# Eight graphs through four message-passing layers on one core: a merge of four edits, with the weighted values ahead of the score products

## The chip, the cores and the metric

The kernel runs on one core of one Trainium2 chip. The metric is the device time of one execution, in microseconds (us). The kernel before takes 3336.92 us, the median of three runs (3333.25 to 3337.58). The core has five engines, each with its own instruction queue: PE (matrix products), DVE (vector), ACT (scalar functions), POOL (GpSimd) and SP, which here issues the DMAs. They meet through semaphores only.

## The reference, cut to what matters

Eight graphs (B = 8) of 1024 nodes with 256 features each pass four layers, each added to `x`:

```python
h = relu(layernorm(x)); x = x + L0(h, adj, nodemask)   # one softmax over the nodes, scales v = h @ Wv
h = relu(layernorm(x)); x = x + L1(h, adj, ...)        # 8 heads of 32: softmax(q k^T * scale * 2 adj) v, then Wo
h = relu(layernorm(x)); x = x + L2(h, adj, ...)        # hypergraph convolutions over (adj != 0)
h = relu(layernorm(x)); x = x + L3(h, adj, ...)        # adj * exp(q k^T), normalised, times v

# L0:  agg = adj @ k;  w = mask / sqrt(256) * sum_d(q * agg);  softmax(w)[:, None] * v
# L1, for one head:
scores = einsum('bhqd,bhkd->bhqk', q, k) * SCALE * (adj + adj)
attn = softmax(scores, axis=-1);  ctx = einsum('bhqk,bhkd->bhqd', attn, v);  out = ctx @ Wo.T + bo
```

Everything is float32.

## The kernel before, in words

The graphs are worked one after the other (`batch`). Seven of them are iterations of a loop in hardware (`Fori`) on DVE, ACT, POOL and SP, the eighth stands behind it as code of its own; PE has all eight in its loop. The order of the work is written out by hand, apart for each engine, and each engine waits on counting semaphores. Nothing is scheduled by a planner.

**The attention loop (L1)** is where most of the change lies. Its 64 *units* are 8 tiles of 128 queries by 8 heads. For a unit `u`:

- PE, `scores(u)`: two products of 128x512 into one of two pairs of PSUM banks (L1104). They are issued in step `u-2`, and wait until DVE has read the pair for unit `u-2`.
- DVE, L726: scores times adjacency into the buffer `Z` (one of three), and the row's maximum into `nm`. It issues in step `u`. DVE then negates that maximum (L731), since ACT adds it as a bias.
- ACT, L912: the exponential in place, with the row sums.
- PE, `transposes(u)`: eight 128x128 transposes of `Z` (L1124), issued in step `u`, into two of three banks that take turns.
- ACT (first half, L904) and DVE (second half, L683) copy them to `PT`, one or two steps later. In every fourth unit (`BOTH = 4`) ACT copies both halves.

Four units (four heads) form a *group* `g`. POOL spreads its inverse sums over columns (L496, `rs`), PE transposes them (`spread_inverses`, L1132, at the end of step 4g+5), and ACT copies the result to `Rs` at the start of step 4g+6 (L909). The weighted values (L1146, 32-column tiles of the array) follow in steps 4g+6 to 4g+8, in parts of 3, 3 and 2 of the 8 key tiles (`PARTS`). The first part waits for `Rs`, since both live in PSUM bank 7. DVE multiplies by `Rs` (L695). After every second group, PE applies the output weights (`project`, through the helper at L983), at the start of steps 8t+14. POOL also computes the 0/1 incidence `H` of a tile in one instruction (L505). The first units run while SP still stacks `kS` and `qS` by DMA.

In one step PE issues: `project` if due, scores of unit u+2, a part of weighted values if due, transposes of unit u, spreading if due:

```python
                    if u + 2 < UNITS:
                        scores(u + 2)
                    for part in range(len(PARTS)):
                        if (g := group_due(u, WEIGH + part)) is not None:
                            weighted_values(g, part)
                    if 0 < u < UNITS:
                        transposes(u)
```

**The start of a graph (L0).** PE transposes the first half of `h` (L1015), four pieces of the adjacency (L1031), and then the second half of `h`, for which it waits until DVE has copied the first half out of PSUM (L594). DVE comes to that copy after it has finished the previous graph. At L0's end the weights of 8 tiles are masked and scaled on DVE (L621), their maximum is taken (L623), broadcast (L625) and transposed by PE.

**From L2 to L3.** PE forms a product of two weight matrices (M3), runs two products whose result nobody reads (`keep_warm`, L1007), and waits for ACT's copy of M3 and for ACT's normalised `h` (L869). `h` waits on DVE's `shift`, which waits on POOL's power (`norm_scale`, L482 and L484); POOL starts this last one behind the layer's last product and a memset (L520).

Of the kernel before, what the change touches and what calls it, by code (L numbers as in the profile page):

```python
# [7 lines left out]
ALU = mybir.AluOpType  # L8
# [23 lines left out]
def build_program(nc, x_in, adj_in, mask_in, wqkT0, wv0, w1attn, bq1, bk1, bv1, bo1,  # L32
# [13 lines left out]
    BOTH = 4  # L46
# [7 lines left out]
    with ctx:  # L54
# [25 lines left out]
        mhalf = sb("mhalf", [P, NT])  # L80
        mask = sb("mask", [P, NT])
# [130 lines left out]
        chain = signal("chain", 9)  # L212
# [86 lines left out]
        PARTS = (3, 3, 2)  # L299
# [168 lines left out]
        def _(pool):  # L468
# [6 lines left out]
            pool.wait_ge(consts_ready.sem, 4)  # L475
# [10 lines left out]
            def batch(b, last):  # L486
# [3 lines left out]
                for g in range(NT * GROUPS):  # L490

                    pool.wait_ge(*invs(b, g + 1))
# [5 lines left out]
                    if g % GROUPS == GROUPS - 1:  # L498

                        t = g // GROUPS  # L500
                        pool.wait_ge(*zs(b, HEADS * (t + 1)))
                        if t == NT - 2:
                            norm_scale(b, 2, 0)
                        stand(pool, waited_pool)
                        pool.tensor_scalar(H[:, t], adjN[:, t], 0.0, 0.0, ALU.is_equal, ALU.is_equal).then_inc(Hs.sem, 1)  # L505
# [26 lines left out]
        def _(dve):  # L532
# [19 lines left out]
            dve.wait_ge(consts_ready.sem, 4)  # L552
# [43 lines left out]
            def batch(b, last):  # L596
# [15 lines left out]
                for t in range(NT):  # L612
                    dve.wait_ge(*agg_ps(b, t + 1))
# [6 lines left out]
                dve.wait_ge(*chain(b, 1))  # L620
                dve.tensor_tensor(sw[:, 1], sw[:, 0], mask16[:], ALU.mult).then_inc(chain.sem, 1)  # L621
                dve.wait_ge(*chain(b, 2))
                dve.reduce_max(s1[:, 0:1], sw[:, 1], AX.X).then_inc(chain.sem, 1)  # L623
                dve.wait_ge(*chain(b, 3))
                dve.tensor_copy(E3[:, 1, 0:P], s1[:, 0:1].broadcast_to([P, P])).then_inc(wm_bc.sem, 1)  # L625
# [3 lines left out]
                dve.reciprocal(s1[:, 3:4], ps[:, 5, 0:1]).then_inc(chain.sem, 1)  # L629
                dve.wait_ge(*chain(b, 4))  # L630
# [703 lines left out]
```

## Time and profile before

| | |
|---|---|
| median of three runs | 3336.92 us |
| the profiled execution | 3340.5 us, span 3337.7 us |
| mean granted PE clock | 0.986 of full speed |
| PE, matmul records | 3172.0 us busy, 95% of the span |
| DVE | 2040.6 us, 61% |
| ACT | 1524.3 us, 46% |
| POOL | 577.5 us, 17% |

A graph takes some 412 us, of which the attention loop is about 150. Shares over the whole span hide that DVE and ACT are idle in the long product stages and nearly full in the attention loop (in 600 to 650 us: PE 49.2, DVE 44.3, ACT 41.2 of 50 us). The records of matmuls overlap, as they are pipelined, so what a product costs PE is read from start to start of neighbouring rows, not from a row's duration. The profiled execution lies 3.6 us above the median.

### The profile page before, as it was taken

What the parts mean: (1) busy time and instruction counts of PE and PEld (TensorE: products, weight loads), DVE (VectorE), ACT (ScalarE), POOL (GpSimd) and SP (SyncE); (2) the same over time, 40 slices, a digit from 0 to 9 for tenths busy, and PEclk for the clock granted to TensorE, in tenths of its full rate; (3) what the DMA queues carried; (4) which work ended last, traced back from release to release, by engine and by line L of the source; (5) the groups of instructions that cost most, each with busy time, mean ns of one, the idle gap of its engine ahead of it and who ended that gap; (6) DMA issues with size and microseconds to landing.
All of it is one profiled execution on the core that took longest, in us unless ns stands there. A gap on an engine that the chain in (4) does not pass through costs nothing.

```text
span 3337.7 us, 64889 instructions
## 1 busy us (share of the span) xinstructions
PE 3172.0 (95%) x23656; PEld 2450.6 (73%) x23656; DVE 2040.6 (61%) x4913; ACT 1524.3 (46%) x2881; POOL 577.5 (17%) x400
## 2 busy tenths in 40 slices
PE   6899998999989999899998999989999899998999
PEld 5677786777867778677776786767867678676786
DVE  2688426884368843687436874378743786437863
ACT  1584215842158431684316833168322683227722
POOL 0123001230012300123001230012300122001320
PEclk8999999999999999999999999999999999999999
DMA  3301203012030020300203002030020301112000
GB/s 109 77 2 33 73 14 77 2 33 73 14 77 2 33 73 14 77 2 33 73 14 77 2 33 73 14 77 2 33 73 18 73 2 43 62 39 52 24 10 13
DMA packets 75103, 135.44 MB, mean 41 GB/s; under 512 B 8592, under 2 KB 43792, under 8 KB 74768
## 3 DMA queue, kind: packets, MB, share of 16 engines
q1 hardware_dynamic: 74768, 131.01, 13.9%
q8 instruction: 206, 3.38, 0.4%
q14 instruction: 129, 1.06, 0.1%
HBM read 72.26 MB, written 8.39 MB: 24 GB/s over the span
## 4 chain that ended last, share of the span: by engine, by line
PE 80%; SPq 7%; issue 4%; DVE 4%; ACT 3%; DMA 1%; POOL 0%; ACTq 0%; DVEq 0%; POOLq 0%
PE ps L983 35%; PE ps L1184 14%; PE ps L1124 14%; SPq L426 7%; PE ps L1146 6%; PE ps L1104 5%; PE ps L1031 2%; PE ps L1132 1%; ACT h L869 1%; DVE hT L594 1%; PE ps L1015 1%; ACT Z L912 1%; DMA qS<-qlo 1%; DVE stats L560 0%; ACT h2T L938 0%
## 5 line engine op out<-in xcount | busy, mean ns | idle before, releaser
L726 DVE CUSTOM_DVE_ANT_0 Z<-ps,adjN 128x1024 f32<-128x1024 f32 x512 | 621.2, 1213 | 64.9 <-PE ps L1104 47.3
L1124 PE MATMUL ps<-ident,Z 128*128 128x128 f32 x4096 | 569.7, 283 | 74.3 <-ACT Z L912 43.6
L912 ACT ACTIVATE Z<-Z,nm 128x1024 f32<-128x1024 f32 x512 | 587.4, 1147 | 29.5 <-DVE nm L731 27.6
L1124 PEld LDWEIGHTS ps<-ident,Z 128*128 128x128 f32 x4096 | 458.7, 143 | 188.6 <-issue 98.5
L904 ACT ACTIVATE PT<-ps 128x512 f32<-128x512 f32 x640 | 364.1, 590 | 84.5 <-PE ps L1124 47.7
L1104 PE MATMUL ps<-kS,qS 128*128 128x512 f32 x1024 | 374.0, 450 | 6.8 <-ACT qS L894 6.8
L1146 PE MATMUL ps<-PT,v 128*32 128x128 f32 x8192 | 303.9, 279 | 0.0
L1146 PEld LDWEIGHTS ps<-PT,v 128*32 128x32 f32 x8192 | 205.6, 110 | 131.9 <-issue 130.7
L683 DVE COPY PT<-ps 128x512 f32<-128x512 f32 x384 | 264.2, 688 | 41.6 <-DMA qS<-qlo 21.7
L496 POOL TENSOR_SCALAR rs<-sm 128x128 f32<-128x128 f32 x128 | 68.2, 533 | 1080.2 <-DVE sm L687 1080.2
L505 POOL TENSOR_SCALAR H<-adjN 128x1024 fp32r<-128x1024 f32 x64 | 233.4, 3646 | 0.0
L983 PE MATMUL ps<-v,P 128*128 128x257 f32 x1024 | 223.6, 380 | 0.0
L983 PE MATMUL ps<-mh,adjT 128*128 128x256 f32 x1024 | 222.3, 380 | 0.0
L983 PE MATMUL ps<-hT,t3T 128*128 128x512 f32 x512 | 221.0, 593 | 0.0
L983 PEld LDWEIGHTS ps<-v,P 128*128 128x128 f32 x1024 | 194.2, 190 | 31.5 <-issue 3.8
L983 PEld LDWEIGHTS ps<-mh,adjT 128*128 128x128 f32 x1024 | 195.1, 191 | 25.9
L482 POOL TENSOR_SCALAR ve<-mv 128x4 f32<-128x4 f32 x80 | 15.7, 197 | 1116.9 <-DVE mv L565 1115.4
L983 PEld LDWEIGHTS ps<-hT,t3T 128*128 128x128 f32 x512 | 97.5, 190 | 118.8 <-issue 118.4
L617 DVE CUSTOM_DVE_ANT_0 E<-ps,G 128x256 f32<-128x256 f32 x64 | 27.2, 425 | 246.5 <-PE ps L983 246.5
L1104 PEld LDWEIGHTS ps<-kS,qS 128*128 128x128 f32 x1024 | 165.8, 198 | 14.6 <-issue 10.0
L983 PE MATMUL ps<-W,hT 128*128 128x256 f32 x768 | 174.3, 381 | 0.0
L966 ACT ACTIVATE E<-ps,cj 128x512 f32<-128x512 f32 x128 | 87.9, 687 | 187.4 <-PE ps L983 187.4
(165 smaller groups left out, 5395.6 us busy)
## 6 DMA issues: line engine op xcount, KB each, us to landing
adjN<-adj_in SPq DMA_DIRECT2D x8, 4096.0 KB, 15.9
kS<-khi SPq DMA_DIRECT2D x48, 256.0 KB, 3.8
kS<-klo SPq DMA_DIRECT2D x48, 256.0 KB, 5.0
qS<-qhi SPq DMA_DIRECT2D x96, 128.0 KB, 3.0
qS<-qlo SPq DMA_DIRECT2D x96, 128.0 KB, 3.1
xn<-x_in SPq DMA_DIRECT2D x8, 1024.0 KB, 6.1
out<-x SPq DMA_DIRECT2D x8, 1024.0 KB, 4.9
W1h<-w1T SPq DMA_DIRECT2D x9, 512.0 KB, 5.7
```

The lines of the kernel that those rows point to most:

```text
L426: sp.dma_start(to.bitcast(F32), src[HD * j:HD * j + HD, :, cols].bitcast(F32)).then_inc(done.sem, 16)
L505: pool.tensor_scalar(H[:, t], adjN[:, t], 0.0, 0.0, ALU.is_equal, ALU.is_equal).then_inc(Hs.sem, 1)
L683: dve.tensor_copy(PT[:, u % PTS, NT // 2:NT], heads_of(ps[:, bank])).then_inc(PT_dve.sem, 1)
L726: dve.tensor_tensor_reduce(Z[:, u % ZS], ps[:, 2 * (u % 2):2 * (u % 2) + 2].rearrange("p a n -> p (a n)"), adjN[:, u // HEADS], SCORE_SCAL ...
L904: act.activation(PT[:, u % PTS, first:first + NT // 2], heads_of(ps[:, bank]), ACT.Copy).then_inc(PT_act.sem, 1)
L912: act.activation(Z[:, u % ZS], Z[:, u % ZS], ACT.Exp, bias=nm[:, u:u + 1], accum_out=sm[:, u:u + 1]).then_inc(exps.sem, 1)
L966: act.activation(E3[:, n % 2], ps[:, n % 4], ACT.Exp, bias=cj[:, n % NT:n % NT + 1]).then_inc(e3s.sem, 1)
L983: mm = pe.matmul(dst, lhsT, rhs, start=(i == 0), stop=(i == len(pairs) - 1))
L1104: mm = pe.matmul(ps[:, 2 * (u % 2) + s], qS[:, hd, rows(t)], kS[:, hd, half(s)], start=True, stop=True)
L1124: mm = pe.transpose(ps[:, turn_bank((u, s)), rows(a)], Z[:, u % ZS, rows(NT // 2 * s + a)], ident[:])
L1146: mm = pe.matmul(ps[HD * j:HD * j + HD, 7, 0:P], v[:, kt, HD * hd:HD * hd + HD], PT[:, (HPG * g + j) % PTS, kt], start=(kt == 0), stop=(kt ...
L1184: mm = pe.matmul(dst(n, i), lhs(n, j, i), rhs(n, j, i), start=(j == 0 and i == 0), stop=(j == NT - 1 and i == 0))
```

## The change

Six things change; the first three are in the attention loop.

1. In a step, PE issues the weighted values ahead of the scores of unit u+2, and they come in two parts of 4 key tiles instead of 3, 3 and 2.
2. The negation of the maxima goes from DVE to POOL (`negate_max`). POOL's order is now written by steps: negate, spread the inverse sums if due, one eighth of a tile's incidence.
3. ACT copies both halves in every sixth unit instead of every fourth; DVE takes the others.
4. L0's start: ACT makes the copies of transposed `h`. PE's second half of `h` waits for the masked `h` (`mhs`) instead of the copies.
5. L0's end: mask and scale are applied by ACT as it copies `G`; the maximum of seven tiles is taken while PE works on the eighth, and DVE then makes maximum and broadcast in one instruction.
6. From L2 to L3: POOL's power and DVE's `shift` of the first half come earlier, ACT normalises the first half ahead of its M3 copy, M3 uses another bank, and the two unread products are gone; the transposes of `h` no longer wait for M3's copy.

```diff
-    BOTH = 4
+    BOTH = 6
-        PARTS = (3, 3, 2)
+        PARTS = (NT // 2, NT // 2)
...
@@ POOL, attention loop
-                for g in range(NT * GROUPS):
...
-                        pool.tensor_scalar(H[:, t], adjN[:, t], 0.0, 0.0, ALU.is_equal, ALU.is_equal).then_inc(Hs.sem, 1)
+                def negate_max(u):
+                    pool.wait_ge(*zs(b, u + 1))
+                    pool.tensor_tensor(nm[:, u:u + 1], nm[:, u:u + 1], minus[:], ALU.mult).then_inc(nms.sem, 1)
...
+                def incidence(t, of):
+                    done = pool.tensor_scalar(H[:, t, of], adjN[:, t, of], 0.0, 0.0, ALU.is_equal, ALU.is_equal)
...
+                for u in range(STEPS):
+                    if u < UNITS:
+                        negate_max(u)
+                    if (g := group_due(u, INVERT)) is not None:
+                        spread_sums(g)
...
+                    if HEADS <= u < UNITS:
+                        incidence(u // HEADS - 1, rows(u % HEADS))
...
@@ POOL, L2 to L3
+                norm_scale(b, 4)
                 pool.wait_ge(*a4_ps(b, NT))
                 stand(pool, waited_pool)
                 pool.memset(v3[:, :, D:HW], 1.0).then_inc(ones_col.sem, 1)
-                norm_scale(b, 4)
@@ DVE, L0
-                hT_copies(b, 0, 0)
                 for n in range(1, NT * NH, 2):
-                    if n == 5:
-                        hT_copies(b, 0, 1)
...
-                dve.tensor_tensor(sw[:, 1], sw[:, 0], mask16[:], ALU.mult).then_inc(chain.sem, 1)
...
-                dve.tensor_copy(E3[:, 1, 0:P], s1[:, 0:1].broadcast_to([P, P])).then_inc(wm_bc.sem, 1)
+                dve.tensor_scalar(E3[:, 1, 0:P], sw[:, 0, NT - 1:NT].broadcast_to([P, P]), s1[:, 0:1], None,
+                                  ALU.max).then_inc(wm_bc.sem, 1)
@@ DVE, attention loop
-                    if u < UNITS:
-                        dve.wait_ge(*zs(b, u + 1))
-                        dve.tensor_scalar(nm[:, u:u + 1], nm[:, u:u + 1], -1.0, None, ALU.mult).then_inc(nms.sem, 1)
@@ ACT
+                hT_copies(0)
                 for n in range(0, NT * NH, 2):
+                    if n == 4:
+                        hT_copies(1)
...
+                normalise(b, 4, x, range(TPH))
                 act.wait_ge(*m3_ps(b, 1))
...
+                normalise(b, 4, x, range(TPH, NT))
@@ PE
-                        pe.wait_ge(*hTs(b, DT))
+                        pe.wait_ge(*mhs(b, NT))
                         transpose_h(b, 0, 1)
...
-                    if u + 2 < UNITS:
-                        scores(u + 2)
                     for part in range(len(PARTS)):
                         if (g := group_due(u, WEIGH + part)) is not None:
                             weighted_values(g, part)
+                    if u + 2 < UNITS:
+                        scores(u + 2)
...
-                keep_warm(bank(1), 2)
+                transpose_h(b, 2, 0)
                 pe.wait_ge(*m3s(b, 1))
-                transpose_h(b, 2, 0)
```

The order of PE's queue before, from the spreading of group 0's inverse sums (end of step 5) through step 7. `kS`, `qS` are the stacked keys and queries, `Z` the exponentials, `PT` their transposes.

```order
L1132 MATMUL ps<-ident,rs 128x128
L1097 REGISTER_ALU
L1104 MATMUL ps<-kS_1,qS_1 128x512 x2
L1146 MATMUL ps<-PT_1,v 32x128 x12
L1117 REGISTER_ALU
L1124 MATMUL ps<-ident,Z_1 128x128 x4
L1115 REGISTER_ALU
L1124 MATMUL ps<-ident,Z_1 128x128 x4
L1097 REGISTER_ALU
L1104 MATMUL ps<-kS_1,qS_1 128x512 x2
L1146 MATMUL ps<-PT_1,v 32x128 x12
```

The scores of units 8 and 9 stand ahead of the two parts of weighted values.

The same stretch of PE's queue after the change:

```order
L1153 MATMUL ps<-ident,rs 128x128
L1167 MATMUL ps<-PT_1,v 32x128 x16
L1118 REGISTER_ALU
L1125 MATMUL ps<-kS_1,qS_1 128x512 x2
L1138 REGISTER_ALU
L1145 MATMUL ps<-ident,Z_1 128x128 x4
L1136 REGISTER_ALU
L1145 MATMUL ps<-ident,Z_1 128x128 x4
L1167 MATMUL ps<-PT_1,v 32x128 x16
L1118 REGISTER_ALU
L1125 MATMUL ps<-kS_1,qS_1 128x512 x2
```

The weighted values stand right behind the spreading, in parts of 16 products, and the scores of units 8 and 9 behind them. The third part, of step 8, is gone.

POOL's queue before, around the first incidence of a graph (`rs` the spread inverse sums, `H` the incidence):

```order
L492 REGISTER_ALU
L496 TENSOR_SCALAR rs<-sm 128x128
L501 ISA
L505 TENSOR_SCALAR H_1<-adjN 128x1024
L492 REGISTER_ALU
```

And after the change (step 8 and part of step 9), with the negations of `nm`:

```order
L495 TENSOR_TENSOR nm<-nm,minus 128x1
L498 REGISTER_ALU
L502 TENSOR_SCALAR rs<-sm 128x128
L507 TENSOR_SCALAR H_1<-adjN 128x128
L494 REGISTER_ALU
L495 TENSOR_TENSOR nm<-nm,minus 128x1
```

Each negation, for which ACT's exponential waits, now stands behind whatever POOL has from the step before.

## Rows read from the trace of the kernel before

**Rows 1.** The page, part 1: engines' busy time, share, instructions.
```profile
PE 3172.0 (95%) x23656; PEld 2450.6 (73%) x23656; DVE 2040.6 (61%) x4913; ACT 1524.3 (46%) x2881; POOL 577.5 (17%) x400
```
**Rows 2.** Timeline, unit 0 of a graph (start us, us, engine, line, what [idle before]).
```profile
536.78 1.14 PE L1104 MATMUL ps<-kS,qS 128*128 128x512 f32 x4 [0.84 <-ACT qS L894]
...
539.12 1.15 ACT L912 ACTIVATE Z<-Z,nm 128x1024 f32<-128x1024 f32 x1 [2.49 <-DVE nm L731]
...
540.42 1.71 PE L1124 MATMUL ps<-ident,Z 128*128 128x128 f32 x8 [2.50 <-ACT Z L912]
```
**Rows 3.** Timeline, eight units of the loop in their steady rhythm, mostly PE.
```profile
620.21 1.03 PE L1124 MATMUL ps<-ident,Z 128*128 128x128 f32 x8
...
621.50 0.28 ACT L909 ACTIVATE Rs<-ps 128x128 f32<-128x128 f32 x1 [1.36 <-PE ps L1132]
...
623.03 1.09 PE L1124 MATMUL ps<-ident,Z 128*128 128x128 f32 x8 [0.25 <-ACT Z L912]
...
623.88 0.71 PE L1104 MATMUL ps<-kS,qS 128*128 128x512 f32 x2
...
624.51 0.86 PE L1146 MATMUL ps<-PT,v 128*32 128x128 f32 x24
...
625.31 1.09 PE L1124 MATMUL ps<-ident,Z 128*128 128x128 f32 x8
...
626.79 0.64 PE L1146 MATMUL ps<-PT,v 128*32 128x128 f32 x16
...
627.37 1.09 PE L1124 MATMUL ps<-ident,Z 128*128 128x128 f32 x8
...
628.22 0.71 PE L1104 MATMUL ps<-kS,qS 128*128 128x512 f32 x2
...
628.76 1.03 PE L1124 MATMUL ps<-ident,Z 128*128 128x128 f32 x8
...
630.03 1.13 PE L983 MATMUL ps<-Wo,ctxn 128*128 128x256 f32 x4
...
638.10 1.03 PE L1124 MATMUL ps<-ident,Z 128*128 128x128 f32 x8
```
**Rows 4.** Timeline of PE at the loop's end, where no scores are left.
```profile
683.72 1.13 PE L983 MATMUL ps<-Wo,ctxn 128*128 128x256 f32 x4
...
684.78 0.86 PE L1146 MATMUL ps<-PT,v 128*32 128x128 f32 x24
...
685.69 1.09 PE L1124 MATMUL ps<-ident,Z 128*128 128x128 f32 x8
...
686.71 0.86 PE L1146 MATMUL ps<-PT,v 128*32 128x128 f32 x24
```
**Rows 5.** Groups by line (xcount | busy, mean ns | idle before, releasers): negation, small POOL operation.
```profile
L731 DVE TENSOR_SCALAR nm<-nm 128x1 f32<-128x1 f32 x512 | 78.8, 154 | 17.8
L482 POOL TENSOR_SCALAR ve<-mv 128x4 f32<-128x4 f32 x80 | 15.7, 197 | 1116.9 <-DVE mv L565 1115.4
```
**Rows 6.** Timeline: DVE's reciprocal and the POOL instruction that waits for it.
```profile
625.64 0.17 DVE L687 RECIPROCAL sm<-sm 128x4 f32<-128x4 f32 x1
626.03 0.54 POOL L496 TENSOR_SCALAR rs<-sm 128x128 f32<-128x128 f32 x1 [4.99 <-DVE sm L687]
```
**Rows 7.** Groups by line: PE's transposes of h, with its idle time before them.
```profile
L1015 PE MATMUL ps<-ident,h 128*128 128x128 f32 x384 | 61.7, 291 | 29.3 <-ACT h L869 15.2 <-DVE hT L594 13.9
```
**Rows 8.** Timeline at a graph's start: DVE's first copy out of the transposes.
```profile
454.50 1.29 DVE L594 COPY hT<-ps 128x512 f32<-128x512 f32 x2
```
**Rows 9.** Stretch behind graph 2's start: busy time by engine, PEclk, DMA share, GB/s.
```profile
868.42:871.83 3.41, 3.41 (x18) 3.41 (x17) 2.37 (x4) 0.60 (x1) 0.00 (x0) 0.50 0.00 0
```
**Rows 10.** Timeline at L0's end: DVE.
```profile
497.40 0.17 DVE L621 TENSOR_TENSOR sw<-sw,mask 128x8 f32<-128x8 f32 x1
...
497.80 0.23 DVE L625 COPY E<-s 128x128 f32<-128x128 f32 x1
```
**Rows 11.** Timeline between L2 and L3: the first product of L3.
```profile
792.72 1.98 PE L983 MATMUL ps<-hT,M 128*128 128x512 f32 x4 [0.94 <-DVE hT L594]
```

More of the change, by code:

```diff
@@ L211, in build_program @@
         wrs = signal("wrs", NT)
-        chain = signal("chain", 9)
+        chain = signal("chain", 8)
         wm_bc = signal("wm_bc", 1)
@@ L612, in batch @@
                 for t in range(NT):
+                    if t == NT - 1:
+                        dve.wait_ge(*wrs(b, NT - 1))
+                        dve.reduce_max(s1[:, 0:1], sw[:, 0, 0:NT - 1], AX.X).then_inc(chain.sem, 1)
                     dve.wait_ge(*agg_ps(b, t + 1))
@@ L629, in batch @@
                 dve.reciprocal(s1[:, 3:4], ps[:, 5, 0:1]).then_inc(chain.sem, 1)
+                dve.wait_ge(*chain(b, 3))
+                dve.tensor_scalar(sw[:, 3], sw[:, 2], s1[:, 3:4], None, ALU.mult).then_inc(chain.sem, 1)
                 dve.wait_ge(*chain(b, 4))
-                dve.tensor_scalar(sw[:, 3], sw[:, 2], s1[:, 3:4], None, ALU.mult).then_inc(chain.sem, 1)
-                dve.wait_ge(*chain(b, 5))
                 dve.wait_ge(*x_free(b, 1))
@@ L808, in batch @@
                 for t in range(NT + 2):
+                    if t == TPH + 3:
+                        shift(b, 4, 0)
                     if t < NT:
@@ L817, in batch @@
                         aggregate(b, 4, t - 2)
-                    if t == TPH + 3:
-                        shift(b, 4, 0)
                 shift(b, 4, 1)
@@ L863, in _, with normalise @@
         def _(act):
-            def normalise(b, l, k, src):
-                for t in range(NT):
+            def normalise(b, l, src, tiles=range(NT)):
+                for t in tiles:
                     if t % TPH == 0:
@@ L872, in batch, with hT_copies @@
             def batch(b, last):
+                def hT_copies(s):
+                    for c in range(DT):
+                        act.wait_ge(*hT_ps(b, s * DT + c + 1))
+                        act.activation(hT[:, c, half(s)], ps[:, 4 + 2 * s + c], ACT.Copy).then_inc(hTs.sem, 1)
+                hT_copies(0)
                 for n in range(0, NT * NH, 2):
+                    if n == 4:
+                        hT_copies(1)
                     act.wait_ge(*aT_ps(b, n + 1))
@@ L879, in batch @@
                     act.wait_ge(*g_ps(b, t + 1))
-                    act.activation(G[:, t], ps[:, 4 + t % 2, 0:D], ACT.Copy).then_inc(gs.sem, 1)
+                    if t == 0:
+                        act.wait_ge(*chain(b, 1))
+                    act.activation(G[:, t], ps[:, 4 + t % 2, 0:D], ACT.Copy, scale=mask16[:, t:t + 1]).then_inc(gs.sem, 1)
                 act.wait_ge(*nwms(b, 1))
-                act.activation(sw[:, 2], sw[:, 1], ACT.Exp, bias=s1[:, 1:2], accum_out=s1[:, 2:3]).then_inc(es.sem, 1)
-                normalise(b, 1, 1, x)
+                act.activation(sw[:, 2], sw[:, 0], ACT.Exp, bias=s1[:, 1:2], accum_out=s1[:, 2:3]).then_inc(es.sem, 1)
+                normalise(b, 1, x)
                 for n in range(2 * GROUPS * NH):
@@ L1257, in batch @@
                 sum_up(*of_nodes(Vh, Vl), (v2s,), [v2s(b, t + 1) for t in range(NT)], a4_ps, tail=4)
-                pe.wait_ge(*x2f(b, 2))
+                pe.wait_ge(*x2f(b, 3))
                 pe.wait_ge(*w3_in(b, 48))
                 for c in range(DT):
-                    mm = product(ps[:, bank(0), D * c:D * (c + 1)], [(W3[:, 1, o, rows(c)], W3[:, 0, o]) for o in range(DT)])
+                    mm = product(ps[:, bank(2), D * c:D * (c + 1)], [(W3[:, 1, o, rows(c)], W3[:, 0, o]) for o in range(DT)])
                 mm.then_inc(m3_ps.sem, 1)
-                keep_warm(bank(1), 2)
+                transpose_h(b, 2, 0)
                 pe.wait_ge(*m3s(b, 1))
-                transpose_h(b, 2, 0)
                 pe.wait_ge(*x2f(b, NT))
```

38 lines of the change are left out of this document (18 added, 20 removed).

## Prediction, made before the changed kernel was run

> **What bounds the kernel now.** I read the page's busy shares first, then the groups by line, and then the timeline of one graph, stage by stage. PE has matmul records in 95% of the span [rows 1], so a term counts only if it moves PE. Those records overlap, so I take PE's costs from start to start. In the attention loop's steady rhythm eight units take 638.10 - 620.21 = 17.89 us [rows 3]. I call the four units of a group A (its transposes stand ahead of the spreading: 620.21, 628.76), B, C and D. A group without output weights takes 628.76 - 620.21 = 8.55, one with them 638.10 - 628.76 = 9.34 [rows 3]. In both PE does its slots back to back but for one wait of 0.25 for B's exponential, in the first (at 623.03).
>
> PE's slots [rows 3, 4]: transposes to scores 0.85 (627.37 to 628.22); scores to transposes 0.54 (628.22 to 628.76); scores to weighted values 0.63 (623.88 to 624.51); 24 product records of weighted values 0.80 (624.51 to 625.31), 16 of them 0.58 (626.79 to 627.37); transposes to weighted values 1.02 (685.69 to 686.71); A's transposes to output weights 1.27 (628.76 to 630.03); output weights to weighted values 1.06 (683.72 to 684.78).
>
> The second number that matters is what a unit needs from its scores on PE to its transposes on PE when nothing else holds it: scores, DVE's multiplication, negation, exponential, transposes. Unit 0 of a graph shows it bare: 540.42 - 536.78 = 3.64 us, each engine waiting for the one before [rows 2]. Before the change it is hidden, since from a unit's scores to its transposes PE has at least this much work: for A, whose scores stand ahead of C's weighted values, 0.63 + 0.80 + 0.85 + 0.63 + 0.58 + 0.85 + 0.54 = 4.88 [rows 3].
>
> **The change in the loop, part by part.** *The order on PE.* A's scores (those of unit u+2 in C's step) now stand behind C's weighted values. From there to A's transposes PE has only C's transposes, D's scores and transposes, scores and A's transposes next: 0.54 + 0.85 + 0.54 + 0.85 + 0.54 = 3.32 us, since D's step has no weighted values left. That is under 3.64. The slack of 1.24 turns into a wait of 0.32, even with DVE's negation. B's, C's and D's scores keep enough work ahead: D's, for one, has 0.54 + 1.02 + 1.02 + 0.54 + 0.85 + 0.54 = 4.51.
>
> *The negation on POOL.* It lies in that same chain. On DVE it takes 0.154 [rows 5] right behind the multiplication. The nearest row for a small POOL operation is 0.197 [rows 5], so +0.04. POOL starts 0.22 after DVE's reciprocal ends (625.64 + 0.17 to 626.03) [rows 6], against some 0.03 on DVE itself, so +0.19. I take +0.23. Bounds: nothing on the near side; on the far side another 0.54, if the negation is caught behind a POOL instruction of the size of L496's [rows 6]. DVE is rid of 0.154 a unit and takes 1/12 of a copy more; that is worth nothing where DVE is not the last, and the chain above has it waiting for A's scores.
>
> *Bank 7.* The first part of weighted values waits for ACT's `Rs`, which starts 621.50 - 620.21 = 1.29 after A's transposes and lasts 0.28 [rows 3]; with about 0.07 for the way to PE (estimate, from 1.30 between the starts of a 1.15 us exponential and the transposes in [rows 2]) PE resumes at 1.64. Before, scores stood in this gap. In a group with output weights those cover it: 1.27 + 1.06 = 2.33.
>
> *The sum for a group.* 32 records of weighted values: 0.80 + (0.80 - 0.58) = 1.02. Without output weights: 1.64 + 1.02 + 0.54 (B's transposes) + 1.02 + 1.02 (to C's weighted values, and those) = 5.24, and from A's scores on 3.64 + 0.23 = 3.87: 9.11 us for 8.55. With them 0.69 more: 9.80 for 9.34. A pair takes 18.91 for 17.89, +1.02. The slot from weighted values to scores has no row; I take it as that to transposes, and it stands twice in a group, so 0.05 either way is worth 11 us in all. This wait can first arise at unit 9, and last at 61: 14 groups, 7 pairs, 7.1 us a graph, **57 us** over eight. The first five units run beside the DMAs that stack `kS` and `qS`, and I leave them as they are. At the loop's end the third part is gone, which may give back up to 0.5 a graph; I count nothing, and keep it for the range.
>
> *What the array's tiling does.* Going from full-array products to 32-column ones costs 0.09 behind scores (0.63 against 0.54) and 0.17 behind transposes (1.02 against 0.85) [rows 3, 4]. The Trainium skill, TensorEngine Tiling (Array Packing), Key Properties, says that changing the tiling mode drains the engine; the rows agree. By counting switches alone, three parts become two and a third of the drains go, which by 0.09 each would make the loop 10 us shorter over the kernel. By the rows the dearer switch takes the place of the cheaper, and nothing is left of it; the sum above has that in its slots.
>
> **The other edits.** L0's start: PE idles 13.9 us in all for DVE's copy of `h` [rows 7], in six of the graphs, since DVE comes late from the previous one (first copy at 454.50, [rows 8]). ACT is free and takes it, so that wait goes. What is late next is DVE's own first copy of the adjacency, which starts where the copy of `h` started; it leaves some 0.3 of each 2.3. I take -12, between 0 and -14. A stretch of 3.41 us at half PE clock stands behind graph 2's start (868.42 to 871.83, PEclk 0.50 [rows 9]) and such a one behind three more of these idle times; if they go, up to 1.7 us each is won. L0's end: DVE's broadcast starts at 497.80, now where the mask product did, at 497.40: 0.40 by eight graphs, **-3** [rows 10]. From L2 to L3: power, shift and ACT's normalising start earlier; the copies of `h` that the first product of L3 waits for (0.94 idle, [rows 11]) are on DVE behind the second half's shift, which moves less. I take 0.8 a graph, **-6**, between 0 and -11. The two unread products are gone there, so PE is idle longer in one piece; where that brings a stretch at half clock as in [rows 9], up to 1.7 us is lost. I set these against the ones won at L0's start, both at nothing. The eighths of incidence on POOL cost nothing on PE: `H` is needed after the loop.
>
> Sum, against the profiled execution's own 3340.5: + 57 - 12 - 3 - 6 = 3376.5. That execution lay 3.6 above the median of the runs, so I predict **3373 us**, 1.1% slower.
>
> **Rivals.**
> - *PE's work alone decides.* If the chain from scores to transposes is hidden after all, for instance because DVE, freed of the negation, starts A's multiplication so early that the 3.32 of PE's work suffice, a group takes 5.24 + 3.32 = 8.56 for 8.55 and 9.25 for 9.34: -0.08 a pair, -4 over the kernel. With -21 from the other edits this gives 3340.5 - 25 - 3.6 = 3312: faster. For it: DVE and POOL are far from full over the span [rows 1]. Against it: unit 0's 3.64 is with all engines empty, and DVE cannot start before the scores are there. It decides from a chain of 3.32 us down.
> - *POOL is late.* The negation stands behind the spreading or the eighth of incidence of the step before. If each critical one is caught for a whole 0.54 [rows 6], 14 groups by 8 by 0.54 add 60: 3433. Against it: in D's step, which has both, DVE finishes its part more than a microsecond ahead of A's maximum. The Trainium skill, SBUF - State Buffer, on the port pair that DVE and GpSimd share, says that a DVE instruction with two SBUF inputs locks GpSimd out; DVE's in the loop read PSUM and one SBUF tensor at most, so by that rule nothing is blocked. No row here shows such a block.
> - *Gains and waits cancel.* With a negation no dearer on POOL than on DVE and slots from weighted values to scores shorter by 0.05, a group takes 5.14 + 3.64 = 8.78 for 8.55 and 9.47 for 9.34: 0.18 on average, 20 us by 14 groups and 8 graphs, against 21 from the other edits: 3336. For it: these are the two prices without a row. Against it: both must err to the same side.
>
> **How the numbers follow.** Forecast 0.72, with its own range 3345 to 3402 (the negation's price from 0.07 to 0.45, the slot by 0.05, the other edits from -8 to -28). PE alone 0.13; POOL late 0.10; cancel 0.05. To leave no more than 2 in 10 out, 3343 to 3404. A measurement of this kernel can tell about 0.2%, 7 us: slower by more 0.83, within 0.04, faster 0.13.
>
> **What would show it.** Right, if in the profile after: A's transposes wait about 0.5 us for ACT's exponential in each group, and DVE waits for A's scores; PE waits for `Rs` ahead of the first part in every other group; eight units take about 18.9 us; PE's wait for copies of `h` at a graph's start is gone. Wrong, if eight units take 17.8, if exponentials wait for POOL by more than half a microsecond beyond that, or if the gain outside the loop is not near 21 us.

## The result, and the profile after

The changed kernel takes 3383.97 us, the median of 4 runs (3378.02 to 3388.48); the kernel before 3337.25 us (4 runs beside them, 3333.25 to 3340.31). The ratio is 1.014, with a 95% interval of 1.012 to 1.0159: slower by 1.4%. The forecast was 3373 us, slower by 1.1%, with a range of 3343 to 3404. The profiled execution of the changed kernel took 3388.48 us, 48.0 more than that of before (3340.5).

The groups of the page after, part 5, for the attention loop (columns: count | busy us, mean ns of one | idle time of the engine before them, and what ended it), the rows that answer to [rows 1, 5]:

```profile
PE 3162.2 (93%) x23624; PEld 2474.5 (73%) x23624; DVE 1956.5 (58%) x4409; ACT 1548.0 (46%) x2865; POOL 745.4 (22%) x1305
...
L739 DVE CUSTOM_DVE_ANT_0 Z<-ps,adjN 128x1024 f32<-128x1024 f32 x512 | 623.5, 1219 | 270.8 <-PE ps L1125 270.8
L1145 PE MATMUL ps<-ident,Z 128*128 128x128 f32 x4096 | 562.2, 281 | 113.9 <-ACT Z L932 74.0
...
L932 ACT ACTIVATE Z<-Z,nm 128x1024 f32<-128x1024 f32 x512 | 587.8, 1148 | 128.9 <-POOL nm L495 128.4
...
L1167 PE MATMUL ps<-PT,v 128*32 128x128 f32 x8192 | 282.4, 280 | 33.8 <-ACT Rs L929 29.4
L495 POOL TENSOR_TENSOR nm<-nm,minus 128x1 f32<-128x1 f32 x512 | 97.5, 190 | 872.2 <-DVE nm L739 872.2
```

PE is less busy, and every engine of the chain waits longer for the one before it: DVE's multiplication for PE's scores (270.8 us, 47.3 before), ACT's exponential for the negation (128.4, 27.6 before), PE's transposes for the exponential (74.0, 43.6 before). The second wait of PE, for `Rs` (29.4 us), is new.

The timeline after, graph 1, nine units of the steady rhythm (start us, us, engine, line, what, [idle before <- who ended it]); it answers to [rows 3]:

```profile
641.30 1.09 PE L1145 MATMUL ps<-ident,Z 128*128 128x128 f32 x8 [0.45 <-ACT Z L932]
...
642.45 1.03 PE L1004 MATMUL ps<-Wo,ctxn 128*128 128x256 f32 x4
...
643.41 1.08 PE L1167 MATMUL ps<-PT,v 128*32 128x128 f32 x32
...
644.42 0.74 PE L1125 MATMUL ps<-kS,qS 128*128 128x512 f32 x2
...
645.00 1.04 PE L1145 MATMUL ps<-ident,Z 128*128 128x128 f32 x8
...
645.96 1.08 PE L1167 MATMUL ps<-PT,v 128*32 128x128 f32 x32
...
646.97 0.74 PE L1125 MATMUL ps<-kS,qS 128*128 128x512 f32 x2
...
647.85 0.54 POOL L502 TENSOR_SCALAR rs<-sm 128x128 f32<-128x128 f32 x1 [0.96 <-DVE sm L700]
647.94 1.23 DVE L739 CUSTOM_DVE_ANT_0 Z<-ps,adjN 128x1024 f32<-128x1024 f32 x1 [0.31 <-PE ps L1125]
...
648.36 0.66 POOL L507 TENSOR_SCALAR H<-adjN 128x128 fp32r<-128x128 f32 x1
...
649.09 0.08 DVE L739 DVE_READ_ACCUMULATOR2_ANT nm<- 128x1 f32 x1
...
649.25 0.19 POOL L495 TENSOR_TENSOR nm<-nm,minus 128x1 f32<-128x1 f32 x1 [0.24 <-DVE nm L739]
...
649.48 1.15 ACT L932 ACTIVATE Z<-Z,nm 128x1024 f32<-128x1024 f32 x1 [0.69 <-POOL nm L495]
...
650.85 1.09 PE L1145 MATMUL ps<-ident,Z 128*128 128x128 f32 x8 [0.45 <-ACT Z L932]
...
652.20 0.28 ACT L929 ACTIVATE Rs<-ps 128x128 f32<-128x128 f32 x1 [0.99 <-PE ps L1153]
...
652.62 1.08 PE L1167 MATMUL ps<-PT,v 128*32 128x128 f32 x32 [0.46 <-ACT Rs L929]
...
660.04 1.09 PE L1145 MATMUL ps<-ident,Z 128*128 128x128 f32 x8 [0.45 <-ACT Z L932]
```

A's transposes stand at 641.30, 650.85 and 660.04. A group with output weights takes 9.55, one without 9.19, the pair 18.74 us for 17.89 before. From A's scores (646.97) to A's transposes (650.85) it is 3.88 us, and each step on the way waits for the one before.

Where the 48 us come from, stage by stage. Each number is worked out from the starts of PE's groups in the two timelines, after less before, summed over the eight graphs:

| stage | forecast | measured |
| --- | --- | --- |
| L0's start | -12 | -19.4 |
| L0's end | -3 | -3.5 |
| loop, first five units | 0 | +1.5 |
| loop, unit 5 to unit 9 | in the 57 | +19.5 |
| loop, unit 9 to 63 | in the 57 | +47.2 |
| loop's end, to the first product of L2 | 0 | -7.4 |
| L2 to L3 | -6 | +9.4 |
| the rest | 0 | +0.9 |
| sum | +36 | +48.2 |

The loop as a whole costs 61 for 57, with its first units, its end and some us of clock in the 61. What the forecast missed on the slow side stands in two places, and in both it is PE's granted clock. At L2 to L3 (it answers to [rows 11]):

```profile
804.04 0.77 PE L1036 MATMUL ps<-ident,h 128*128 128x128 f32 x5 [0.16 <-ACT h L879]
...
805.30 1.29 DVE L610 COPY hT<-ps 128x512 f32<-128x512 f32 x2 [0.29 <-issue]
...
806.64 3.35 PE L1004 MATMUL ps<-hT,M 128*128 128x512 f32 x4 [1.83 <-DVE hT L610]
```

and behind the wait for the DMA that stacks `qS`, in unit 5:

```profile
563.54 0.60 ACT L924 ACTIVATE PT<-ps 128x512 f32<-128x512 f32 x1 [3.61 <-DMA qS<-qlo]
...
564.20 0.66 PE L1145 MATMUL ps<-ident,Z 128*128 128x128 f32 x4 [3.48 <-ACT PT L924]
...
565.71 1.94 PE L1167 MATMUL ps<-PT,v 128*32 128x128 f32 x32 [0.46 <-ACT Rs L929]
```

The busy times of two stretches (us; PE, PEld, DVE, ACT, POOL, each with its count; then PEclk, DMA share, GB/s), in the form of [rows 9]:

```profile
807.11:810.52 3.41, 3.41 (x8) 1.63 (x7) 0.00 (x0) 0.49 (x2) 0.00 (x0) 0.50 0.03 5
564.77:571.60 6.83, 6.37 (x69) 5.01 (x71) 2.64 (x6) 5.09 (x9) 0.44 (x3) 0.50 0.00 0
```

In both the granted clock is at its lower level (1.2 of 2.4 GHz): the product that took 1.98 takes 3.35, the 32 records of weighted values 1.94 for 1.08. Before the change no stretch at half clock stood at L3's first product; after it one stands there in all eight graphs, 34.1 us together. In six of the eight it begins already in PE's idle time, up to 0.8 us ahead of the product, in the other two up to 0.5 behind the product's start. Behind unit 5 there were 30.7 us, and there are 54.6. Behind L0's start there were four stretches (13.7 us), and there is none.

### The profile page after: what moved, and what is told of

It reads as the page before. It is cut to its first block, busy times and chain, and to the rows that moved or that the text cites. A ratio compares the mean times of both kernels' runs of the same rounds, so it can differ in the third digit from the quotient of the medians.

```text
span 3386.5 us, 65469 instructions
## 1 busy us (share of the span) xinstructions
PE 3162.2 (93%) x23624; PEld 2474.5 (73%) x23624; DVE 1956.5 (58%) x4409; ACT 1548.0 (46%) x2865; POOL 745.4 (22%) x1305
## 3 DMA queue, kind: packets, MB, share of 16 engines
q14 instruction: 123, 1.01, 0.1%
## 4 chain that ended last, share of the span: by engine, by line
PE 57%; issue 14%; DVE 12%; SPq 7%; POOL 4%; ACT 3%; DMA 1%; DVEq 1%; POOLq 0%; ACTq 0%
PE ps L1004 32%; PE ps L1205 10%; SPq L427 7%; PE ps L1145 5%; PE ps L1167 5%; PE ps L1125 3%; DVE junk L775 2%; POOL H L507 2%; DVE stats L576 2%; DVE PT L696 2%; PE ps L1053 1%; PE ps L1153 1%; DVE dn L784 1%; ACT Z L932 1%; POOL rstd L486 1%
## 5 line engine op out<-in xcount | busy, mean ns | idle before, releaser
L739 DVE CUSTOM_DVE_ANT_0 Z<-ps,adjN 128x1024 f32<-128x1024 f32 x512 | 623.5, 1219 | 270.8 <-PE ps L1125 270.8
L1145 PE MATMUL ps<-ident,Z 128*128 128x128 f32 x4096 | 562.2, 281 | 113.9 <-ACT Z L932 74.0
L1145 PEld LDWEIGHTS ps<-ident,Z 128*128 128x128 f32 x4096 | 483.3, 144 | 235.6 <-DVE PT L696 63.5
L932 ACT ACTIVATE Z<-Z,nm 128x1024 f32<-128x1024 f32 x512 | 587.8, 1148 | 128.9 <-POOL nm L495 128.4
L924 ACT ACTIVATE PT<-ps 128x512 f32<-128x512 f32 x592 | 341.0, 590 | 78.5 <-DMA qS<-qlo 28.0
L696 DVE COPY PT<-ps 128x512 f32<-128x512 f32 x432 | 294.7, 682 | 46.8 <-DMA qS<-qlo 26.7
L507 POOL TENSOR_SCALAR H<-adjN 128x128 fp32r<-128x128 f32 (+1 forms) x456 | 318.7, 699 | 0.0
L1167 PE MATMUL ps<-PT,v 128*32 128x128 f32 x8192 | 282.4, 280 | 33.8 <-ACT Rs L929 29.4
L495 POOL TENSOR_TENSOR nm<-nm,minus 128x1 f32<-128x1 f32 x512 | 97.5, 190 | 872.2 <-DVE nm L739 872.2
L1167 PEld LDWEIGHTS ps<-PT,v 128*32 128x32 f32 x8192 | 216.2, 111 | 85.7 <-issue 79.6
```

Of the source, the lines that this page charges most:

```text
L495: pool.tensor_tensor(nm[:, u:u + 1], nm[:, u:u + 1], minus[:], ALU.mult).then_inc(nms.sem, 1)
L507: done = pool.tensor_scalar(H[:, t, of], adjN[:, t, of], 0.0, 0.0, ALU.is_equal, ALU.is_equal)
L696: dve.tensor_copy(PT[:, u % PTS, NT // 2:NT], heads_of(ps[:, bank])).then_inc(PT_dve.sem, 1)
L739: dve.tensor_tensor_reduce(Z[:, u % ZS], ps[:, 2 * (u % 2):2 * (u % 2) + 2].rearrange("p a n -> p (a n)"), adjN[:, u // HEADS], SCORE_SCAL ...
L924: act.activation(PT[:, u % PTS, first:first + NT // 2], heads_of(ps[:, bank]), ACT.Copy).then_inc(PT_act.sem, 1)
L932: act.activation(Z[:, u % ZS], Z[:, u % ZS], ACT.Exp, bias=nm[:, u:u + 1], accum_out=sm[:, u:u + 1]).then_inc(exps.sem, 1)
```

## Experiments

Twelve kernels ran. A ratio is that to the kernel before, run on the same chip. "A pair" is a pair of groups, eight units, from the median over the graphs of the time from unit 9 to unit 61, divided by 6.5: 17.89 before, 18.72 after (the one pair in the timeline above takes 18.74). The edits are cut to what matters; if nothing else is said they are made to the changed kernel.

**Scores first again.** Theory: the order on PE is what makes the loop slow.

```
+                    if u + 2 < UNITS:
+                        scores(u + 2)
                     for part in range(len(PARTS)):
...
-                    if u + 2 < UNITS:
-                        scores(u + 2)
```

> The changed kernel with scores issued ahead of the weighted values again; parts of 4 and 4, POOL's negation and all else as changed. Theory (the chain from A's scores to A's transposes, 3.87 us, waits because only 3.32 us of PE's work stand in front of it): from A's scores PE now has 0.63 + 1.02 + 0.85 + 0.54 + 0.85 + 0.54 = 4.43 us, the wait ahead of A's transposes goes, eight units take 17.3 to 17.6 us (18.74 in the changed kernel, 17.89 before), and the kernel takes about 3295 us, faster than before. Rival (POOL's negation or its late turn costs by itself, in whatever order PE issues): eight units stay above 18.2 us and the kernel above 3350.

Measured: 3287.82 us, ratio 0.9856 (0.9839 to 0.9872); a pair takes 17.10. That is below the 17.3 to 17.6 that were expected, and by which slot is open. One reordered statement is worth 96 us, more than the whole loss. Groups of 8.83 and 8.16 us in the timeline of this kernel:

```profile
620.40 1.09 PE L1145 MATMUL ps<-ident,Z 128*128 128x128 f32 x8
...
629.23 1.03 PE L1145 MATMUL ps<-ident,Z 128*128 128x128 f32 x8
...
637.39 1.09 PE L1145 MATMUL ps<-ident,Z 128*128 128x128 f32 x8
```

**The order alone, on the kernel before** (the same exchange made there, three parts, negation on DVE).

> The kernel before with the weighted values (parts 3, 3, 2) ahead of the scores, and nothing else. Theory: PE has 4.07 us between A's scores and A's transposes against a chain of 3.64, so there is no wait there; what is left is the wait for Rs that scores no longer cover and the dearer switches: 8.87 for 8.55 and 9.56 for 9.34, 0.54 a pair, about 3367 us. Rival (only the chain matters, the rest is moved work): 3337.

Measured: 3372.17 us, ratio 1.0112 (1.0092 to 1.0132); a pair takes 18.29. The order alone costs 0.40 a pair, 22.0 us from unit 9 to 61. Another 10.0 stand between units 5 and 9, where 17 us more are at half clock.

**Three parts.** `PARTS = (3, 3, 2)` again, in the changed kernel.

> The changed kernel with parts of 3, 3 and 2 key tiles, still ahead of the scores. Theory: D's step has weighted values again, so from A's scores to A's transposes PE has 0.54 + 1.02 + 0.58 + 0.54 + 0.85 + 0.54 = 4.07 us, over 3.87: the wait goes, although a third switch of the tiling is paid. By slots a group takes 8.87 and 9.56, a pair 18.43, and the kernel about 3367 us. Rival (the number of parts, each with its switch, is what costs): a pair above 18.74 and the kernel above 3390.

Measured: 3349.56 us, ratio 1.0042 (1.0028 to 1.0057); a pair takes 18.04, where 18.43 was expected. With three parts more of PE's work lies between A's scores and A's transposes, since D's step has a part of its own: from the ones to the others it is 4.03 us in this kernel, over the chain's 3.88, and the wait is gone. The group without output weights takes 8.86, as expected (8.87); the one with them takes 9.20 for 9.56. So what was priced too dear is the output weights, from A's transposes to the first weighted values: 2.06 for 2.33.

**Scores first with three parts.** What is left of the loop's change is the negation on POOL and the copies dealt out anew.

> The changed kernel with the scores ahead of the weighted values, and the weighted values in parts of 3, 3 and 2 key tiles as before. It differs from the kernel before, in the loop, by everything but these two edits: the negation on GpSimd and the copies dealt out anew. Theory (merging the parts into two is what makes scores-first with two parts faster than before, 17.10 for 17.89 a pair of groups): 17.9 a pair, median near 3288 + 51 = 3339 less some 7. Rival (the relief of VectorE does it, the parts do not matter): 17.1 a pair, median near 3288.

Measured: 3327.97 us, ratio 0.9973 (0.9962 to 0.9983); a pair takes 17.89, as before. The expectation had 3339 less some 7. With the four kernels above and the one before, the loop's three changes come apart (us a pair):

| | scores first | weighted values first |
| --- | --- | --- |
| three parts, as before on DVE and POOL | 17.89 | 18.29 |
| three parts, DVE relieved | 17.89 | 18.04 |
| two parts, DVE relieved | 17.10 | 18.72 |

Merging the parts gains 0.79 in one column and costs 0.68 in the other. Relieving DVE (the negation on POOL, against a few more copies) is worth nothing with scores first and 0.25 with weighted values first. That 0.25 is not the chain: with three parts A's scores to A's transposes take 4.02 us without the relief and 4.03 with it. It stands at the output weights, which wait for DVE's copy of `PT`. The order alone, on the kernel before:

```profile
650.03 1.03 PE L1124 MATMUL ps<-ident,Z 128*128 128x128 f32 x8
...
650.58 0.69 DVE L683 COPY PT<-ps 128x512 f32<-128x512 f32 x1
...
651.32 1.13 PE L983 MATMUL ps<-Wo,ctxn 128*128 128x256 f32 x4
...
652.38 0.86 PE L1146 MATMUL ps<-PT,v 128*32 128x128 f32 x24
```

And with DVE relieved (three parts, weighted values first):

```profile
649.96 1.03 PE L1145 MATMUL ps<-ident,Z 128*128 128x128 f32 x8
...
650.16 0.69 DVE L696 COPY PT<-ps 128x512 f32<-128x512 f32 x1
...
651.06 1.03 PE L1004 MATMUL ps<-Wo,ctxn 128*128 128x256 f32 x4
...
652.02 0.86 PE L1167 MATMUL ps<-PT,v 128*32 128x128 f32 x24
```

In the first the copy ends at 651.27 and the output weights start at 651.32; in the second it has ended at 650.85.

**The negation back on DVE.**

```
-                    pool.tensor_tensor(nm[:, u:u + 1], nm[:, u:u + 1], minus[:], ALU.mult)
...
+                        dve.tensor_scalar(nm[:, u:u + 1], nm[:, u:u + 1], -1.0, None, ALU.mult)
```

> The changed kernel with the negation back on DVE; POOL keeps the spreading and the eighths of incidence. Theory: the chain goes from 3.87 to 3.64 us and stays the last, so eight units go from 18.74 to about 18.3 us, and the kernel from 3384 to about 3358. Rival (the weighted values' place alone, by PE's slots and the wait for Rs, makes the loop longer): no change, 3384.

Measured: 3374.6 us, ratio 1.012 (1.0103 to 1.0137); a pair takes 18.89, not less but more. Two rows of its timeline bound the chain, a third shows what is late in its place:

```profile
643.89 0.74 PE L1129 MATMUL ps<-kS,qS 128*128 128x512 f32 x2
...
647.68 1.09 PE L1149 MATMUL ps<-ident,Z 128*128 128x128 f32 x8 [0.36 <-ACT Z L936]
...
658.30 1.13 PE L1008 MATMUL ps<-Wo,ctxn 128*128 128x256 f32 x4 [0.20 <-DVE PT L697]
```

The chain is 3.79 long, only 0.09 shorter than with POOL. And the output weights now wait for DVE's copy of `PT`, which the negations have pushed back. So POOL is not what lengthens the chain, and the expectation of 3358 failed on a price: the forecast had POOL at 0.23 more, and it is 0.09. That the median is still 9 us below the changed kernel's comes from outside the steady loop: from unit 9 to 61 it needs 8.1 more over the graphs, but from L2's last product on 16.2 less, since the stretch at half clock is there in one graph only.

**Work put into the wait, and beside it.** The test of the bound itself: two unread products a group, ahead of B's scores, which lie between A's scores and A's transposes, or ahead of A's scores.

```
+                    if u >= 8 and u % HPG == 2:      (the other kernel: == 1)
+                        for _ in range(2):
+                            pe.matmul(ps[:, 2 * (u % 2), 0:P], ident[:], ident[:], start=True, stop=True)
                     for s in range(NH):
```

> The changed kernel with two more products in each group of four units: identity by identity, 128 by 128, written into the bank of B's scores just ahead of these scores and overwritten by them (their result is used nowhere). They stand in D's step, between A's scores and A's transposes. Each is estimated at 0.21 us from eight transposes of that size in 1.09 and rows of 0.77 for longer ones, so 0.43 a group and 112 groups make 48 us of TensorE work. Theory (TensorE waits in front of A's transposes: the chain from A's scores takes 3.88 and the work beside it 3.32): the two products go into that wait, the loop stays within 0.1 of 18.74 a pair of groups, and the median within 10 us of 3384. Rival (TensorE's own work bounds the group): the pair grows by 0.86 and the median is near 3432.

> The same two unread products a group, put into C's step just ahead of A's scores, where the chain has not begun. Theory (the group is bounded by TensorE's work outside the chain plus the chain): nothing hides them, the pair of groups grows by about 0.86 to 19.6, and the median is near 3384 + 48 = 3432. Rival (the place does not matter, the wait in front of A's transposes takes up any 0.43 of work): within 10 us of 3384.

Measured: 3376.28 us, ratio 1.0116 (1.0094 to 1.0139), with the products inside the chain's time, a pair 18.72; 3432.18 us, ratio 1.0283 (1.026 to 1.0305), with the same products ahead of it, a pair 19.62. In the first kernel, A's transposes at both ends of a pair, and the products:

```profile
617.95 1.09 PE L1148 MATMUL ps<-ident,Z 128*128 128x128 f32 x8
...
625.07 0.61 PE L1126 MATMUL ps<-ident 128*128 128x128 f32 x4
...
636.69 1.09 PE L1148 MATMUL ps<-ident,Z 128*128 128x128 f32 x8
```

In the second:

```profile
620.79 1.09 PE L1148 MATMUL ps<-ident,Z 128*128 128x128 f32 x8 [0.45 <-ACT Z L932]
...
626.12 0.71 PE L1126 MATMUL ps<-ident 128*128 128x128 f32 x4
...
640.44 1.09 PE L1148 MATMUL ps<-ident,Z 128*128 128x128 f32 x8 [0.45 <-ACT Z L932]
```

18.74 as without them, and 19.65. The same work is free in one place and costs 48 us in the other, within 8 us of what the theory said for each. That shows that between A's scores and A's transposes the chain decides, and ahead of A's scores PE's own work. The rest of a group was not tested this way; in the group without output weights PE also waits 0.46 for `Rs`.

**The edit from L2 to L3 alone, on the kernel before**, with its earlier power, shift and normalising.

> The kernel before with only the edits between L2 and L3 (earlier power and shift, ACT's order, M3's bank, unread products gone). By the trace of the changed kernel this stretch, with the half clock in it, is 0.97 us longer a graph: 3345 us, 8 more than before. Rival (it is shorter as predicted, and what the changed kernel shows there is an echo of the clock in the loop): 3331.

Measured: 3329.68 us, ratio 0.9978 (0.9967 to 0.9989). The expectation was wrong and its rival right: there is no stretch at half clock behind L3's first product here, and the edit gains 1.0 us a graph (8.19 to 7.20, from the last product of L2 to the second half's transposes of `h`). The same place in this kernel:

```profile
788.29 0.77 PE L1016 MATMUL ps<-ident,h 128*128 128x128 f32 x5 [0.16 <-ACT h L869]
...
789.19 1.29 DVE L594 COPY hT<-ps 128x512 f32<-128x512 f32 x2
...
790.53 1.98 PE L984 MATMUL ps<-hT,M 128*128 128x512 f32 x4 [1.47 <-DVE hT L594]
```

DVE starts its copy 0.90 us after the first half's last group of transposes, where in the changed kernel it is 1.26 (804.04 to 805.30), so PE's idle time is 1.47 for 1.83, and the edit gains 0.36 less there. The changed kernel with the negation back on DVE has 1.48 as well; why the negation on POOL makes DVE late at this place no run shows.

**Unread products there**, in the changed kernel: two of 128 by 512 ahead of the transposes of `h`, as the kernel before had them, or in the gap ahead of L3's first product.

```
                mm.then_inc(m3_ps.sem, 1)
+                keep_warm(bank(1), 2)
                transpose_h(b, 2, 0)
```

> The changed kernel with the two unread products back ahead of the first transposes of h for L3, where they stood before. Theory (PE's sparse work there brings a stretch at half clock, 3.4 to 6.8 us long, in each graph, and it costs 1.5 to 2.4 us): the half clock does not come, L2 to L3 is shorter by about 2 us a graph, 3369 us. Rival (the gap of 1.83 us behind the transposes, which stays, is what brings it): 3384 and the half clock still there.

```
-                pe.wait_ge(*m3s(b, 1))
                 pe.wait_ge(*x2f(b, NT))
+                keep_warm(3, 2)
+                pe.wait_ge(*m3s(b, 1))
```

> The changed kernel with two unread products in the gap of 1.83 us between the transposes of h and the first product of L3. Theory (the gap brings the half clock): gone, about 15 to 19 us less, 3367 us. Rival (the sparse transposes before it bring it): as changed, 3384.

Measured: 3365.6 us (ratio 1.0084, 1.0064 to 1.0104) and 3366.46 us (1.0088, 1.0069 to 1.0108). In both the stretches at L3's first product are gone, and 18 us with them. Of these 15.0 and 15.2 stand at the place itself, a little under half of the 34.1; the rest stands mostly in units 5 to 9. On whichever side of the transposes the products stand, they take the half clock away; a theory by which only one of the two places helps falls. From the last product of L2 to the second half's transposes it is 7.56 us a graph with either (7.36 and 7.18 in the last graph). It is 7.56 also in seven graphs of the kernel with scores first and three parts, which has the same idle time of 1.83, no unread products and no stretch in those graphs; in the changed kernel it is 8.84 to 9.32. So the loss there was the clock.

**Both repairs: scores first, and two unread products in the gap.**

> The changed kernel with scores first, as in the first of these, and with two unread products of 512 columns in the gap between the transposes of h and the first product of L3. Theory: what scores first gives (3295), and the stretch at half clock at L3's start gone as well, some 15 to 19 us: about 3278. Rival (the half clock there costs nothing that the gap doesn't): 3295.

Measured: 3274.97 us, ratio 0.9815 (0.9799 to 0.9832).

**The same, and products in two more idle times of PE**, three ahead of the second half of unit 5's transposes and two ahead of unit 0's.

```
+                        if (u, s) == (5, 1):
+                            keep_warm(7, 3)
                         wait_bank((u, s))
...
                     if u == 0:
+                        keep_warm(7, 2)
                         transposes(u)
```

> The best version so far (scores ahead of the weighted values, two unread products in the gap ahead of L3's first product) with more unread products of 128 by 512 in two further idle times of TensorE, written into a bank that nothing uses then: three ahead of the second half of unit 5's transposes (about 2.6 us of a wait of 3.5 for the copy of PT behind the DMA of qS) and two ahead of unit 0's transposes (about 1.7 of a wait of 2.6). In the version before, 40.8 us at half clock in all follow each of these places. Theory (an idle TensorE is what the half clock follows, and its own work is the bound in both stretches): both kinds of stretch go, and with them up to 20 us behind unit 5, where the work is back to back, and half as much or less behind unit 0, where transposes and scores still wait for exponentials: 3245 to 3255. Rival (the stretches go, but other engines set the pace there, or they come back a few units later): 3275, and within 0.3% of the version before.

Measured: 3259.34 us, ratio 0.9762 (0.9746 to 0.9779), the fastest of all. The wait for the DMA is filled:

```profile
543.34 2.74 PE L1028 MATMUL ps<-adjT,ident 128*128 128x512 f32 x6
...
545.91 0.61 PE L1147 MATMUL ps<-ident,Z 128*128 128x128 f32 x4
```

The stretches behind unit 5 are gone (41.0 us at half clock, now none), and units 5 to 9 take 15.4 us less over the graphs. Behind unit 0 17.1 us are left of 41.0, and the time there is as it was (+0.8): there PE waits for exponentials and for ACT's copies of `PT`, and a slow PE costs nothing that shows. So the theory held behind unit 5 and its rival behind unit 0, and the whole lies just outside the 3245 to 3255 expected.

## Why the prediction was right, and where it was not

*The mechanism.* The chain from A's scores to A's transposes takes over where PE's work is 3.32. It was forecast at 3.87 and is 3.88; the pair of groups at 18.91 and is 18.74. The two kernels with unread products show the bound directly.

*Two errors in the chain cancelled.* Unit 0's bare 3.64 [rows 2] was too short for the loop by about 0.15. Its multiplication, in the timeline of before:

```profile
537.67 1.23 DVE L726 CUSTOM_DVE_ANT_0 Z<-ps,adjN 128x1024 f32<-128x1024 f32 x1 [3.14 <-PE ps L1104]
```

From scores to the multiplication it is 0.97 in the loop (646.97 to 647.94) against 537.67 - 536.78 = 0.89 here, and from the exponential to the transposes 1.37 (649.48 to 650.85) against 1.30 [rows 2]. POOL's negation was too dear by about as much: 0.23 was taken, and with the chain measured at 3.79 and 3.88 it is 0.09. That the sum of the two came out within 0.01 is luck. What was mis-sized is POOL's start. It comes 0.08 after DVE has written its maximum (649.09 + 0.08 to 649.25), not the 0.22 that [rows 6] show behind a reciprocal; its 0.190 was foreseen from 0.197 [rows 5].

*PE's slots.* The wait for `Rs` was put at 1.64 and is 1.77 (650.85 to 652.62). Output weights to the first weighted values: 2.33 forecast, 2.11 measured (641.30 to 643.41). Those two are why the group with output weights came out at 9.55 for 9.80 and the other at 9.19 for 9.11. The 2.33 was added from slots of the kernel before, in which the output weights start just as DVE's copy of `PT` ends; with DVE relieved they start 1.15 after A's transposes for 1.27, and the weighted values 0.96 after them for 1.06. The size of the parts does not do it: 24-record parts follow the output weights in 1.06 (651.32 to 652.38) and in 0.96 (651.06 to 652.02). The forecast put the relief of DVE at nothing, since it looked at the chain alone.

*What the loop's edges gave.* The end of the loop was left at nothing with up to 0.5 a graph kept for the range; it gave 7.4 us, 0.9 a graph. The 13 groups from unit 9 to 61 cost 45.0 where the forecast has 53. Units 5 to 9 hold the first of the 14 groups and cost 19.5. The granted clock is at half for 23.9 us more there. In the two graphs in which it is at half for as long before and after, these units cost 1.82 and 1.38, which for eight graphs is some 13 and leaves 7 for the clock; by the last experiment (15.4 for 41.0) the clock would be 9. So 10 to 13 are the loop, against 4 for one group, and what makes this first stretch so dear is open. That the 14 groups come to the forecast's 57 or close to it, by 45 and 10 to 13, is again two errors that cancel.

*The other edits.* L0's start: -12 forecast, -19.4 measured. PE's idle time in front of the transposes of `h` fell by 13.2 ([rows 7]: 29.3, and 16.1 after), as forecast; the rest fits the four stretches at half clock that went (13.7 us at half, so an estimate of 6.8). L0's end: -3 and -3.5. L2 to L3: -6 forecast. Without the clock it is close to that: from the last product of L2 on, the changed kernel with scores first and three parts, which has the half clock in one graph only, needs 0.6 a graph less than the kernel before (median of the graphs), some 5 in all. With the half clock it is +9.4. The row of the whole group after:

```profile
L1036 PE MATMUL ps<-ident,h 128*128 128x128 f32 x384 | 62.6, 290 | 16.1 <-ACT h L879 15.6
```

*The step that failed* is "I set these against the ones won at L0's start, both at nothing". Won are 6.8, lost 15 at L3's first product and 7 to 9 behind unit 5, some 16 net. The forecast named the risk from [rows 9] and set it against the four stretches at L0's start; it came in all eight graphs at one place, and a place where stretches already stood grew worse. Less the 7.4 of the loop's end, and with some 4 in small terms, that is the 12 between 36 and 48. Part of it cancelled, so the total came out nearer than its terms. The profile of before did not show how many would come.

*The rivals.* "PE's work alone decides" is refuted by the free products; had PE's work alone decided, they would have cost 48 us. "POOL is late": it is not. In all 512 units of the changed kernel the negation starts 0.08 to 0.09 us after DVE has written its maximum, so it is never caught. It is close: POOL's spreading is over (647.85 + 0.54 = 648.39) and the eighth of incidence (0.66 from 648.36) at 649.02, while DVE writes its maximum from 649.09. From unit 9 on the margin is nowhere under 0.09, and the "more than a microsecond" of the forecast is not there. "Gains and waits cancel" needed shorter slots from weighted values to scores; these are 1.01 for the 1.02 forecast.

*What stays open.* Why the half clock comes at L3's first product in some kernels and graphs and not in others. Six kernels have an idle time of 1.83 there in the first seven graphs and of 1.45 in the last. Of the seven graphs with 1.83 it came in 7 (the changed kernel), 7 (products ahead of A's scores), 6 (scores first), 6 (three parts), 5 (products ahead of B's scores) and none (scores first with three parts). With 1.45, in the last graph, it came in four of these six. Two more kernels, the edit alone on the kernel before and the negation on DVE, have 1.47 in the first seven graphs, and there it came in none of the 14; in their last graphs (1.44 and 1.45) it came in one. So the length of the idle time alone does not settle it: 31 of 42 graphs with 1.83, 5 of 8 with 1.45, none of 14 with 1.47. The Trainium skill, TensorE: Matmul & The Clock Gate, Part 1, says that the monitor behind the clock runs freely and is not set back by a kernel, so that the moment of a change depends on how the work falls against it. That would fit such counts; no run here shifts the place alone in time, so it is not shown.

## What to carry to other kernels

Before a statement is moved on the bottleneck engine, add up that engine's own work between each unit's start of its chain and the instruction that needs the chain's end, and take the smallest of these sums, not the mean: here one unit in four had 3.32 us for a chain of 3.88, and the merged parts, a gain of 0.79 in the other order, took the cover from just that unit. Then test it with free work: products that nobody reads cost nothing where the chain decides and their full price where the engine does. And an idle time of the bottleneck engine that something else sets is to be looked at for what the clock does behind it: unread products in three such places took 29 us (3287.8 to 3259.3), beside the 48 by which the changed kernel with scores first is faster than the kernel before, the edits at L0 included.

## What the runs showed of the hardware

- The granted clock fell in or just behind an idle time of 1.83 us between transposes and products in 31 of 42 graphs of six kernels; seven of the eleven without it are those of one kernel. With products in three idle times and the scores first, the mean granted clock of the run was 0.995, for 0.976 in the changed kernel.
- What a stretch at half clock costs depends on what decides there: 41.0 us behind unit 5 cost 15.4, 34.1 at L3's first product 15.0, and taking 24 of 41.0 away behind unit 0 gave nothing that shows.
- The Trainium skill, TensorEngine Tiling (Array Packing), Key Properties, says that changing the tiling mode drains the engine. Counted by switches, two parts for three should help in either order. It does in one (17.89 to 17.10) and hurts in the other (18.04 to 18.72), where the wait for the chain is larger than what the switches give. How much of the 0.79 gained is the switch no run separates; the slots have 0.63 from scores to weighted values for 0.54 to transposes [rows 3].
- A 128x1 operation on POOL in a chain behind DVE costs 0.09 more than on DVE itself (3.88 for 3.79), though it takes 0.190 for 0.154.
